# Batches 2 to 6: ScalarE's paired side pieces set in two steps of the scan each, and none in a step in which ScalarE scales a diverted sum

## The chip, the cores and the metric

One core of one Trainium2 chip runs the whole kernel in one launch. The metric is the device time of the launch in microseconds; lower is better. The five engines used are TensorE (PE), VectorE (DVE), ScalarE (ACT), GpSimd (POOL) and SyncE (SP, which only starts DMAs). Each runs its own list of instructions in order, and they meet at semaphores.

## The reference, cut to what matters

The input is 8 sequences of 512 tokens of width 512, in fp32. For each sequence:

```python
xz = einsum('bld,ed->bel', hidden, in_proj_w)      # x and z, 1024 channels each
x = silu(conv(x, 4 taps) + conv_b)
dt_lo, B, C = split(x_proj_w @ x)                  # 32, 16, 16
delta = softplus(dt_proj_w @ dt_lo + dt_proj_b)
for n in 16 states:                                # a scan over the 512 tokens
    h[n] = h[n] * exp(delta * A[:, n]) + delta * B[n] * x
    y += h[n] * C[n]
y = (y + x * D) * silu(z)
x1 = layernorm(hidden + out_proj_w @ y)
out = layernorm(x1 + mixture_of_experts(x1))       # 8 experts, 2 of them per token
```

The experts work on tokens that are sorted by expert: rows are scattered to DRAM, loaded tile by tile, multiplied, stored, and gathered again.

## The kernel before, in words

A batch is one sequence. The scan of a batch is cut in 128 **steps**: step 8n+j is state n (0 to 15) of channel block j (0 to 7), one VectorE scan of 128x512. (The change's own words call such a step a row; here "rows" is kept for lines of the profile.) Batches 2 to 6 share one plan, `SEG_FULL`; batch 0 uses `SEG_PRO`, batch 1 `SEG_TWO`, batch 7 `SEG_EPI`, and the change leaves those three alone. What a step does on each engine:

- **ScalarE**: `decay` (L1784), dA = exp(delta * A) into one of two PSUM buffers. Decay r overwrites the buffer of scan r-2, so it waits until scan r-2 is done. Then, in 7 steps of a batch, `scale_part` (L1767), and then the step's side pieces.
- **GpSimd**: the product dbu (L1925), then its side pieces.
- **VectorE**: in even steps it first adds a sum of the previous transposes to y (`state_part`, L1965, 128x1024), then scan r (L1976), which needs decay r and dbu r, then its side pieces.
- **TensorE**: in even steps it transposes a part of a finished state (L1334, 8 transposes) into one of two buffers hTp; the sum of two steps later reads it. Before that part it waits (`turned_taken`) until ScalarE has taken every side transpose of the earlier steps out of these same buffers.

Of the 64 sums of a batch, 7 are diverted (`BY_DMA`): ScalarE scales the part (128x1024) and a DMA adds it to y, and VectorE skips that sum. The steps of these are 14, 30, 46, 62, 78, 94 and 110.

The **side pieces** are all the other work of three batches at once: the projections and gates of the next batch, the output projection, routing and experts of the one before. `plan` simulates the engines with costs written by hand and returns, for each engine, the list of (step, piece). Each engine works through its own list in order, and where it comes to a piece that is not ready, it stands. ScalarE's pieces that matter here:

- `z i` (exp and copy of a projected gate tile out of PSUM, L1660 and L1666, the copy frees the bank), `z2 i` (ln and exp, L1671 and L1678);
- `x j` (first tap of the convolution from PSUM to u, L1574; VectorE's piece `x j`, L1996, adds the other three taps and frees the bank);
- `sig j` (exp, L1585), `sig2 j` (ln and exp, L1590 and L1597), after which GpSimd multiplies (L1857) and the projection `xproj` on TensorE can start once all eight are done (ScalarE takes it out of PSUM at L1601);
- `dt j` (abs and relu from PSUM, L1624 and L1632; the relu frees the bank), `dt2 j` (exp and ln, L1636 and L1642);
- `ln1 t`, `ln2 t` (three 128x1 operations, `rs`, and the normalization L1544);
- `yT`, `x1T`, `xsT`, `xsL`, `yinit` (copies of side transposes out of hTp, L1684, L1682, L1686, L1680, L1604); `moe`, `moeL` (L1746), `scale` (L1734), `skip` (L1615).

The pairs in brackets run back to back: in a coarse plan such as `SEG_FULL` the first half of a piece calls the second (`if not w.seg.fine: piece(w, ("sig3", j))`). In the fine plans (batches 0 and 1) each half is planned as a piece of its own.

ScalarE's list in the plan of before, where the prediction follows it (a bracket is one step, in order; a star marks a step with `scale_part`):

```
13 [moeL 12, xsL 13]   14* [yT 1]   15 []   16 [xsL 14]
38 []   39 [z 0, z2 0]   40 []   41 [yT 4, yT 5, z 1]
44 [sq2 0]   45 [sum2 1, ln2 0]   46* []   47 [sq2 1, z 2]
51 [sq1 2, z2 2]   52 [ln1 2]   53 [z 3]
72 [x 1, sig 0, sig2 0]   73 [scale 0, sig 1, sig2 1, x 2]
77 [sig 3, sig2 3]   78* [scale 5, x 5, sig 4]
79 [sig2 4, scale 6, x 6, sig 5, sig2 5]   80 [x 7, sig 6, wT]
81 [sig2 6, scale 7, sig 7, sig2 7]   82 []
93 [dt 1, skip 2]   94* [dt2 1]   95 [moe 0]   96 [skip 3]
97 [moe 1, yinit 2, yinit 3]   98 []   99 [dt 2, xsT 2, xsT 3, dt2 2]   100 []
109 [moe 4, dt 5]   110* []   111 [xsT 6, yinit 4, dt2 5]
```

VectorE's pieces there: `x 2` in step 73, `x 5` in 77, `x 6` in 78, `x 7` in 79, each after the scan of its step. TensorE's side transposes: `yT 1` in step 12, `yT 4, 5` in 38, `yinit 2, 3` in 94, `xsT 2, 3` in 96, `yinit 4` in 108.

Of the kernel before, what the change touches and what calls it, by code (L numbers as in the profile page):

```python
# [41 lines left out]
STEPS = NS * ND  # L42
NH = NT
# [45 lines left out]
def last_den(t):  # L89
# [4 lines left out]
SINGLE = {"z": ("z", "z1"), "z2": ("z2", "z3"), "zb": ("zb", "zb1"), "zb2": ("zb2", "zb3"), "sig2": ("sig2", "sig3"), "dt": ("dt", "dt1"), "dt2": ("dt2", "dt3"),  # L94
          "ln1": ("rs1", "ln1"), "ln2": ("rs2", "ln2"), "lnF": ("rsF", "lnF")}
# [253 lines left out]
BY_DMA = [NH * n + 2 for n in range(NS) if n % 2 == 0 and n < NS - 2]  # L349


def by_dma(q, halved=False):

    return not halved and q in BY_DMA
# [170 lines left out]

class Segment:

    def __init__(self, pieces, pace, blocks, next_blocks, steps=STEPS):
        self.fine = any(x[0] in ("dt1", "rs1") for x in pieces)
        self.shares = FINE_SHARES if self.fine else SHARES  # L530
        order, users, turns = plan(pieces, steps, pace, steps > STEPS, self.fine)
# [16 lines left out]
        if steps == STEPS and not self.fine:  # L548
            order["pool"] += [(row + AHEAD - 1, ("hold",) + x, 0) for row, x, _ in order["dve"] if x[0] in STILL and row + AHEAD <= steps]
        self.ends_with_tile = [x for row, x, _ in order["act"]][-1:] == [("moe", LATE - 1)]  # L550
# [185 lines left out]
def build(nc, hid, hidT, w_inT, conv_w, conv_b, w_xT, w_dtT, dt_b, A_log, D, w_outT, gateT, w_expT, exp_b, ident_c, before_c, ramp_c, out):  # L736
    with ExitStack() as ctx:
# [27 lines left out]
        rows = sb("rows", [P, L])  # L765
# [38 lines left out]
        row = sb("row", [P, NT, NE])  # L804
# [710 lines left out]
        def _(act):  # L1515
# [30 lines left out]
            def piece(w, x):  # L1546
                name = x[0]
# [38 lines left out]
                elif name == "sig2":  # L1586
# [4 lines left out]
                    if not w.seg.fine:  # L1591
                        piece(w, ("sig3", j))
# [23 lines left out]
                elif name == "dt":  # L1616
# [8 lines left out]
                    if not w.seg.fine:  # L1625
                        piece(w, ("dt1", j))
# [6 lines left out]
                elif name == "dt2":  # L1633
# [3 lines left out]
                    if not w.seg.fine:  # L1637
                        piece(w, ("dt3", j))
# [8 lines left out]
                elif name in ("z", "zb"):  # L1647
# [13 lines left out]
                    if not w.seg.fine:  # L1661
                        piece(w, (name + "1", i))
# [4 lines left out]
                elif name in ("z2", "zb2"):  # L1667
# [4 lines left out]
                    if not w.seg.fine:  # L1672
                        piece(w, (name[:-1] + "3", i))
# [22 lines left out]
                elif name == "ln1":  # L1696
                    if not w.seg.fine:
                        piece(w, ("rs1", x[1]))
# [9 lines left out]
                elif name == "ln2":  # L1708
                    if not w.seg.fine:
                        piece(w, ("rs2", x[1]))  # L1710
# [28 lines left out]
                elif name in ("moe", "moeL"):  # L1739
                    rows, stored, count = results_of(w, x[1], w.e if name == "moe" else w.d)  # L1740
# [6 lines left out]
                elif name == "wT":  # L1747
                    first, end_t, _ = group_of(x)
# [448 lines left out]
```

## Time and profile before

| | us |
|---|---|
| median of 3 runs (2259.15 to 2264.75) | 2264.38 |
| the profiled execution | 2260.66 |
| its span, first to last instruction | 2258.9 |
| mean length of batches 2 to 6, first scan to first scan | 260.6 |

| engine | busy us | share of the span |
|---|---|---|
| PE | 2036.0 | 90% |
| DVE | 1982.8 | 88% |
| POOL | 1854.5 | 82% |
| ACT | 1658.4 | 73% |

A line of the timeline reads: start in the span, duration, engine, line of the kernel, operation, out<-in, shapes, count (equal neighbours are merged), and in brackets how long the engine stood idle before it and what ended that. Consecutive ScalarE or VectorE operations overlap a little, so what one of them costs is the distance from its start to the next start. The five batches of `SEG_FULL` start at 561.2, 822.1, 1084.6, 1345.1 and 1604.9 us and end at 1864.2; batch 3 (822.1 to 1084.6) is used as the pattern below.

### The profile page before, as it was taken

The page shows a single profiled execution, that of the slowest core. Times are in us where ns is not written, and L with a number is a line of the kernel's source. Part 1 is how long each engine was busy: PE and PEld are TensorE (multiplying, and loading weights), DVE is VectorE, ACT ScalarE, POOL GpSimd, SP SyncE. Part 2 cuts the span into 40 slices and gives each one's busy share as a digit, 9 for nine tenths or more (in the row PEclk, how much of TensorE's full clock was granted, in tenths as well). Part 3 has the DMA queues.
Part 4 walks back from the last instruction along what each step waited for, and adds up shares of the span by engine and source line. Part 5 has one row for each costly group of instructions (what it writes and reads, how often), then busy time and mean ns, then how long its engine had stood idle before and what let it go on. Part 6 is the DMA issues. An engine that isn't in the chain of part 4 may idle for free. (4 is left out here: it accounts for less than half of the span.)

```text
span 2258.9 us, 30428 instructions
## 1 busy us (share of the span) xinstructions
PE 2036.0 (90%) x8624; PEld 1200.9 (53%) x8624; DVE 1982.8 (88%) x2191; ACT 1658.4 (73%) x3074; POOL 1854.5 (82%) x1505
## 2 busy tenths in 40 slices
PE   8897779898999989999899998999899998879898
PEld 3444455455564555545555555645556455655453
DVE  5899989989999999899999999899998998989912
ACT  5767858767598866979588875988678886667534
POOL 2988999788998889889898889989898997696503
PEclk9897879989899999999999999999999999789999
DMA  5432142367754786557863678557855576495775
GB/s 164 160 108 70 40 148 77 95 212 229 246 126 124 231 289 180 137 171 233 280 172 106 209 249 264 118 153 248 293 150 136 176 245 236 146 272 189 246 270 117
DMA packets 222085, 412.79 MB, mean 183 GB/s; under 512 B 29880, under 2 KB 36152, under 8 KB 221920
## 3 DMA queue, kind: packets, MB, share of 16 engines
q1 hardware_dynamic: 180448, 322.36, 42.6%
q0 software_dynamic: 20496, 57.16, 12.4%
q10 hardware_dynamic: 20976, 31.33, 4.3%
q8 instruction: 72, 1.18, 0.2%
q14 instruction: 93, 0.76, 0.1%
HBM read 299.37 MB, written 85.72 MB: 170 GB/s over the span
## 5 line engine op out<-in xcount | busy, mean ns | idle before, releaser
L1784 ACT ACTIVATE dA<-delta,negA 128x512 f32<-128x512 f32 (+1 forms) x1146 | 714.4, 637 | 317.4 <-DVE hst L1976 250.1
L1925 POOL TENSOR_TENSOR hst<-u,Bbc 128x512 f32<-128x512 f32 x666 | 880.7, 1427 | 57.4 <-PE hTp L1334 36.3
L1976 DVE TENSOR_TENSOR_SCAN hst<-dA,hst 128x512 f32<-128x512 f32 x672 | 790.3, 1207 | 44.0 <-ACT dA L1784 36.8
L1334 PEld LDWEIGHTS hTp<-ident,hst 128*128 128x128 f32 x4096 | 496.2, 149 | 318.4 <-issue 172.2
L1334 PE MATMUL hTp<-ident,hst 128*128 128x128 f32 x4096 | 557.9, 288 | 96.5 <-DVE hst L1976 24.4
L1965 DVE SCALAR_TENSOR_TENSOR y<-hTp,Ct,y 128x1024 f32<-128x1024 f32 x463 | 585.1, 1264 | 54.5 <-PE hTp L1334 51.6
L1925 POOL TENSOR_TENSOR first_dbu<-u,Bbc 128x512 f32<-128x512 f32 x222 | 295.1, 1411 | 16.5 <-DVE hits L2057 11.6
L1976 DVE TENSOR_TENSOR_SCAN hst<-dA,first_dbu 128x512 f32<-128x512 f32 x224 | 263.2, 1207 | 17.7 <-issue 9.1
L1318 PE MATMUL bank<-wslot,hidT 128*128 128x512 f32 x512 | 250.3, 621 | 8.1 <-ACT zs L1666 6.2
L1318 PE MATMUL bank<-wslot,tokT 128*128 128x512 f32 x496 | 233.3, 598 | 4.0 <-ACT tokT L1686 3.9
L1318 PE MATMUL bank<-delta,tokT 128*128 128x512 f32 x480 | 224.4, 600 | 0.0
L1318 PE MATMUL bank<-hidT,wslot 128*128 128x512 f32 x384 | 178.1, 601 | 13.6 <-DVE u L1996 13.5
L1996 DVE SCALAR_TENSOR_TENSOR u<-bank,cw,u 128x511 f32<-128x511 f32 (+2 forms) x192 | 142.8, 744 | 31.0 <-ACT u L1574 25.8
L1318 PEld LDWEIGHTS bank<-wslot,hidT 128*128 128x128 f32 x512 | 94.2, 199 | 93.0 <-issue 82.7
L1318 PEld LDWEIGHTS bank<-wslot,tokT 128*128 128x128 f32 x496 | 87.9, 191 | 91.0 <-issue 91.0
L1318 PEld LDWEIGHTS bank<-delta,tokT 128*128 128x128 f32 x480 | 87.1, 195 | 80.0 <-issue 80.0
L1318 PEld LDWEIGHTS bank<-hidT,wslot 128*128 128x128 f32 x384 | 68.6, 191 | 96.3 <-issue 61.5
L1933 POOL TENSOR_TENSOR first_dbu<-u,Bbc 128x512 f32<-128x512 f32 x64 | 82.6, 1348 | 43.2 <-DMA Bbc<-b_scratch 23.4
L1857 POOL TENSOR_TENSOR u<-u,side 128x512 f32<-128x512 f32 x64 | 84.1, 1320 | 38.4 <-ACT side L1597 38.3
L1746 ACT ACTIVATE ysb<-bank 128x512 f32<-128x512 f32 x116 | 68.3, 589 | 62.1 <-PE bank L1318 53.8
L1872 POOL TENSOR_TENSOR zs<-zs,side 128x512 f32<-128x512 f32 x64 | 98.4, 1538 | 16.7 <-ACT side L1678 16.6
L1318 PE MATMUL bank<-wslot,side 128*128 128x512 f32 x224 | 106.5, 601 | 1.9 <-ACT side L1680 1.6
(187 smaller groups left out, 2886.7 us busy)
## 6 DMA issues: line engine op xcount, KB each, us to landing
wslot<-in_w_expT SPq DMA_DIRECT2D x90, 1024.0 KB
Bbc<-b_scratch SPq DMA_DIRECT2D x113, 256.0 KB
wslot<-in_w_inT SPq DMA_DIRECT2D x26, 1024.0 KB
y<-scaled POOLq DMA_DIRECT2D x49, 512.0 KB
zs<-sorted_tokens ACTq DMA_DIRECT2D x91, 256.0 KB, 6.1
sorted_results<-ysb SPq DMA_DIRECT2D x90, 256.0 KB
res<-in_w_expT SPq DMA_DIRECT2D x18, 1024.0 KB, 5.7
gate_scratch<-zs SPq DMA_DIRECT2D x64, 256.0 KB, 2.8
```

The lines of the kernel that those rows point to most:

```text
L1318: mm = nc.tensor.matmul(dst, lhs(k), rhs(k), start=(k == 0), stop=(k == n - 1))
L1334: mm = nc.tensor.transpose(hTp[q % 2][:, tok(j)], hst[n % 2][:, j, start:start + P], ident[:, :])
L1746: nc.scalar.activation(rows, ps[:, :], ACT.Copy).then_inc(bank_taken[s], 1)
L1784: nc.scalar.activation(decay_of(step, halved), delta[w.odd][:, j, cols], ACT.Exp, scale=negA[:, j, n:n + 1]).then_inc(exp_done, 1)
L1857: nc.gpsimd.tensor_tensor(x_j, x_j, side[j % 2][:, :], ALU.mult).then_inc(x_ready, 1)
L1872: nc.gpsimd.tensor_tensor(zs[i % 2][:, :], zs[i % 2][:, :], side[i % 2][:, :], ALU.mult).then_inc(z_ready, 1)
L1925: nc.gpsimd.tensor_tensor(dbu_row(n, j), u[w.odd][:, j, :], Bbc[n % 2][:, :], ALU.mult).then_inc(dbu_done, 1)
L1933: nc.gpsimd.tensor_tensor(half_dbu[k % 4].rearrange("p (k t) -> p k t", k=2), u[w.odd][:, j:j + 2, cols], Bbc[n % 2][:, cols].unsqueeze(1) ...
L1965: nc.vector.scalar_tensor_tensor(y_part, hTp[q % 2][:, :], Ct[odd][:, t, n:n + 1], y_part, ALU.mult, ALU.add).then_inc(acc_done, 1)
L1976: nc.vector.tensor_tensor_scan(hst[n % 2][:, j, :], dA[j % 2][:, :], dbu_row(n, j), 0.0, ALU.mult, ALU.add).then_inc(scan_done, 1)
L1996: tap = nc.vector.scalar_tensor_tensor(late, bank[s][:, 0:L - k], cw[:, j, TAPS - 1 - k:TAPS - k], late, ALU.mult, ALU.add)
```

## The change

The list that the planner made for ScalarE in `SEG_FULL` is rewritten after planning, by `one_by_one`: a piece whose planned step scales a diverted sum moves to the next step; a pair becomes two pieces, the second one step later than the first, unless the list is already behind (then it stays in the same step); and the order of the list is kept, so that a piece behind a moved one is moved with it. The lists of the other engines, and the planner's model, stay as they were. The calls by which the first half of a pair runs the second are switched off in these batches too (`w.seg.single`).

```diff
+SCALED_ROWS = [2 * (q + NH + 1) for q in BY_DMA]
...
+def one_by_one(pieces, steps):
+
+    rows, last = [], 0
+    for row, x, _ in pieces:
+        row += row in SCALED_ROWS
+        for k, name in enumerate(SINGLE.get(x[0], (x[0],))):
+            last = min(max(row + k * (last <= row), last), steps - 1)
+            rows.append((last, (name,) + x[1:], 0))
+    return rows
...
         self.fine = any(x[0] in ("dt1", "rs1") for x in pieces)
+        self.single = self.fine or steps == STEPS
...
+        if self.single and not self.fine:
+            order["act"] = one_by_one(order["act"], steps)
...
-                    if not w.seg.fine:
+                    if not w.seg.single:
                         piece(w, ("sig3", j))
```

The last edit is made at seven places: for `sig3`, `dt1`, `dt3`, `z1`/`zb1`, `z3`/`zb3`, `rs1` and `rs2`.

## Rows read from the trace of the kernel before

**Rows 1.** Busy time of each engine in batch 3 (windows; columns as in its first line).
```profile
core 0: us, PE busy (x) PEld busy (x) DVE busy (x) ACT busy (x) POOL busy (x), PEclk, DMA share, GB/s
822.10:1084.60 262.50, 246.47 (x1070) 146.51 (x1069) 240.81 (x250) 206.74 (x374) 235.57 (x192) 0.95 0.64 198
```

**Rows 2.** VectorE's waits in batches 2 to 6: total us, times, longest.
```profile
DVE hst L1976 <- ACT dA L1784: 35.6, 42, 1.7
DVE y L1965 <- PE hTp L1334: 28.1, 52, 1.0
```

**Rows 3.** ScalarE idle before decays, batches 2 to 6 (line 1784): ended by, us, times.
```profile
  DVE hst L1976: 164.2, 204
```

**Rows 4.** ScalarE's timeline in steps 78 and 79 of batch 3.
```profile
980.30 0.71 ACT L1734 ACTIVATE spare<-res,mix 128x512 f32<-128x512 f32 x1
980.91 0.76 ACT L1574 ACTIVATE u<-bank,cb,cw 128x512 f32<-128x512 f32 x1
...
982.09 0.68 ACT L1784 ACTIVATE dA<-delta,negA 128x512 f32<-128x512 f32 x1
982.70 0.62 ACT L1590 ACTIVATE side<-side 128x512 f32<-128x512 f32 x1
983.36 0.63 ACT L1597 ACTIVATE side<-side 128x512 f32<-128x512 f32 x1
983.89 0.71 ACT L1734 ACTIVATE zs<-res,mix 128x512 f32<-128x512 f32 x1
```

**Rows 5.** VectorE's timeline in steps 77 and 78 of batch 3.
```profile
980.61 1.22 DVE L1976 TENSOR_TENSOR_SCAN hst<-dA,hst 128x512 f32<-128x512 f32 x1
981.74 2.29 DVE L1996 SCALAR_TENSOR_TENSOR u<-bank,cw,u 128x511 f32<-128x511 f32 x3
983.95 1.21 DVE L1976 TENSOR_TENSOR_SCAN hst<-dA,hst 128x512 f32<-128x512 f32 x1
```

**Rows 6.** ScalarE's timeline in step 99 of batch 3.
```profile
1029.98 0.68 ACT L1632 ACTIVATE delta<-bank,dtb 128x512 f32<-128x512 f32 x1
...
1030.55 1.08 ACT L1686 ACTIVATE tokT<-hTp 128x512 f32<-128x512 f32 x2
```

**Rows 7.** VectorE's timeline in steps 98 to 100 of batch 3.
```profile
1029.21 1.28 DVE L1965 SCALAR_TENSOR_TENSOR y<-hTp,Ct,y 128x1024 f32<-128x1024 f32 x1 [0.47 <-PE hTp L1334]
1030.41 2.33 DVE L1976 TENSOR_TENSOR_SCAN hst<-dA,hst 128x512 f32<-128x512 f32 x2
1033.30 1.28 DVE L1965 SCALAR_TENSOR_TENSOR y<-hTp,Ct,y 128x1024 f32<-128x1024 f32 x1 [0.56 <-PE hTp L1334]
```

**Rows 8.** TensorE's timeline in steps 96 and 98 of batch 3.
```profile
1031.29 1.10 PE L1318 MATMUL bank<-res,tokT 128*128 128x512 f32 x2 [1.24 <-ACT tokT L1686]
1032.22 1.91 PE L1334 MATMUL hTp<-ident,hst 128*128 128x128 f32 x16
```

**Rows 9.** TensorE's and then VectorE's timeline after step 14 of batch 3.
```profile
848.65 1.94 PE L1334 MATMUL hTp<-ident,hst 128*128 128x128 f32 x8 [2.44 <-ACT tokT L1684]
...
850.63 1.28 DVE L1965 SCALAR_TENSOR_TENSOR y<-hTp,Ct,y 128x1024 f32<-128x1024 f32 x1 [0.28 <-PE hTp L1334]
```

**Rows 10.** TensorE (step 40) and VectorE (steps 46, 53, 73) of batch 3, timeline.
```profile
895.33 1.94 PE L1334 MATMUL hTp<-ident,hst 128*128 128x128 f32 x16 [0.39 <-ACT tokT L1684]
...
905.14 1.22 DVE L1976 TENSOR_TENSOR_SCAN hst<-dA,hst 128x512 f32<-128x512 f32 x1 [1.42 <-ACT dA L1784]
...
919.22 1.22 DVE L1976 TENSOR_TENSOR_SCAN hst<-dA,hst 128x512 f32<-128x512 f32 x1 [0.91 <-ACT dA L1784]
...
968.20 1.53 DVE L1996 SCALAR_TENSOR_TENSOR u<-bank,cw,u 128x511 f32<-128x511 f32 x2 [1.57 <-ACT u L1574]
```

**Rows 11.** TensorE at the start of xproj (batch 5) and ScalarE at its end.
```profile
1521.21 2.81 PE L1318 MATMUL bank<-u,hidT 128*128 128x512 f32 x6 [1.29 <-POOL u L1857]
...
1530.11 0.59 ACT L1601 ACTIVATE rows<-bank 64x512 f32<-64x512 f32 x1 [1.11 <-PE bank L1318]
```

**Rows 12.** TensorE's timeline at the part of step 110 of batch 3.
```profile
1054.41 1.06 PE L1334 MATMUL hTp<-ident,hst 128*128 128x128 f32 x8 [0.34 <-ACT y L1604]
```

More of the change, by code:

```diff
@@ L1624, in piece @@
                     nc.scalar.activation(a, ps[:, :], ACT.Abs, bias=dtb[:, j:j + 1]).then_inc(sp_step, 1)
-                    if not w.seg.fine:
+                    if not w.seg.single:
                         piece(w, ("dt1", j))
@@ L1636, in piece @@
                     nc.scalar.activation(a, a, ACT.Exp, scale=-1.0).then_inc(sp_step, 1)
-                    if not w.seg.fine:
+                    if not w.seg.single:
                         piece(w, ("dt3", j))
@@ L1660, in piece @@
                     nc.scalar.activation(a, ps[:, :], ACT.Exp, scale=-1.0).then_inc(zsig_step, 1)
-                    if not w.seg.fine:
+                    if not w.seg.single:
                         piece(w, (name + "1", i))
@@ L1671, in piece @@
                     nc.scalar.activation(a, a, ACT.Ln, bias=1.0).then_inc(zsig_step, 1)
-                    if not w.seg.fine:
+                    if not w.seg.single:
                         piece(w, (name[:-1] + "3", i))
@@ L1696, in piece @@
                 elif name == "ln1":
-                    if not w.seg.fine:
+                    if not w.seg.single:
                         piece(w, ("rs1", x[1]))
@@ L1708, in piece @@
                 elif name == "ln2":
-                    if not w.seg.fine:
+                    if not w.seg.single:
                         piece(w, ("rs2", x[1]))
```

## The prediction

> **What bounds the kernel now.** I read the windows first: in batch 3, VectorE is busy 240.8 of 262.5 us, more than ScalarE (206.7) and GpSimd (235.6) [rows 1]; TensorE's 246.5 is modelled and holds matmuls that wait for banks. So VectorE sets the pace, step by step, and what counts is its idle time, 21.7 us in this batch. The waits say what ends it: over batches 2 to 6, 35.6 us in 42 waits are for a decay dA from ScalarE, 28.1 us in 52 are for transposed parts from TensorE [rows 2]. The first is what the change can touch: at most 7.1 us of a batch.
>
> The third view speaks against it. ScalarE stands before its decays 164.2 us in 204 waits, for VectorE's scan [rows 3]. So in a third of the 640 steps ScalarE is as far ahead as two dA buffers allow. There, a side piece that stands before a decay runs in time in which ScalarE would wait anyway; the same piece behind that decay starts only after scan r-2. Splitting does not spread work over idle time, it pushes it behind a gate. Whether that costs depends on who waits for the piece.
>
> **The change, part by part.** It adds and removes no instruction (batches 2 to 6, 32 pairs in each). Costs of ScalarE from start to start: decay 0.61, scale 0.61 (980.30 to 980.91, 982.09 to 982.70), second half of `sig2` 0.53, taken as 0.54 (983.36 to 983.89) [rows 4]; relu of `dt` 0.57, two copies of transposes 1.08 [rows 6]. A first tap takes 0.76 to its end [rows 4].
>
> *Decays that come earlier (gain).* In step 46 VectorE waits 1.42 us, in step 53 0.91 us [rows 10]. Step 46: `ln2 0`'s second half leaves step 45, so decay 46 comes earlier; but it then stands between decay 46 and decay 47, and decay 47 comes no earlier. Nothing is gained there. Step 53: `ln1 2`'s normalization leaves step 52; the 0.91 go. Against this, step 40: `z 0` now has one operation in step 39 and three in step 40, behind a decay that waits for scan 38; `yT 4` and `yT 5`, in step 41, come about 1.1 us later, and TensorE's part started 0.14 us after them (895.33, released by the copy) [rows 10], with only 0.3 or so to spare for VectorE's sum: a loss of 0.8. What is left, some 0.1 to 0.5 us gained, meets step 73: there VectorE waits 1.57 us for `x 2` [rows 10], and `x 2` moves to step 74, behind one more decay (0.61). I take steps 37 to 76 together as 0; ends: 1.5 us gained if the losses are covered, 1 us lost if the gain is.
>
> *Step 15.* `yT 1` leaves the starred step 14 and runs behind decay 15. TensorE's next part started when that copy was out, and VectorE's sum waited for the part, 0.28 us [rows 9]. The copy comes one decay later: +0.6 us, and the earlier decay 15 buys nothing, since the sum is later.
>
> *Steps 77 and 78, the largest term.* Follow `one_by_one`: `sig2 3` gives its second half to step 78, so `scale 5`, `x 5` and `sig 4` (moved out of the starred step) stand in 79; then `sig2 4` is split, and `scale 6`, `x 6` and all behind stand in 80. VectorE's list was not touched: it wants `x 5` in step 77 and `x 6` in step 78. So VectorE, having done scan 77, waits for a piece that stands behind decay 79, which waits for scan 77. No one is deadlocked, but nothing overlaps: after scan 77 come decay 0.61, scale 0.61, tap 0.76 and two hand-overs of 0.03 to 0.05: 2.1 us idle, where now the taps start the moment the scan is over (981.74) [rows 5]. Then after scan 78: decay 0.61, second half of `sig2 4` 0.54, scale 0.61, tap 0.76, hand-overs: 2.6, of which 0.1 exists now (the scan ends at 985.16, 983.95 + 1.21 [rows 5]): 2.5 us. `x 7` is not late: three taps and scan 79 (2.29 + 1.2 [rows 5]) cover its 3.3 us of ScalarE. Sum +4.6 us. Bounds: not below 4.0, since both chains hang on VectorE's own scans; up to 6 if TensorE, idle meanwhile, is slow after it.
>
> *Step 82, xproj.* `sig3 6`, `scale 7`, `sig 7` and `sig2 7` stand behind decay 82, which waits for scan 80, where four of them ran before it. Eight gates must be multiplied before `xproj`; TensorE starts it at the moment the last is out (1.29 us of waiting, released by GpSimd) and ScalarE waits 1.11 us for its end [rows 11]. I work out that the last gate comes 2.3 us later; the parts of two steps that lie between cover some of it at step 88: +1.5 us, between 0 (in batches in which TensorE was late itself) and 2.3.
>
> *Steps 96 to 100.* With `dt 1`'s relu moved behind decay 94 its bank comes free later, ScalarE idles before decay 94 and has some 1.1 us more to do before `yinit 3`, for which part 96 waits: sum 98, which waits 0.47 us already [rows 7], is later by 1.2. Then step 99: only `dt 2`'s first half is left in it; the relu, `xsT 2` and `xsT 3` stand behind decay 100, which waits for scan 98. After that scan: decay 0.61, relu 0.57, copy 0.6 [rows 4, 6], matmuls of the expert tile 0.93 (1031.29 to 1032.22, started by the copy) [rows 8], part until its sum 1.08 (1032.22 to 1033.30) [rows 7, 8]: 3.8 to 3.9 us, of which scan 99 (1.13) covers its share: 2.8 idle where 0.56 is now [rows 7]: +2.2. Bounds of both together: 1.5 to 4.
>
> *Steps 106 to 112.* Decay 109 and the starred step 110 get `dt1 4` to `dt3 4` and `dt1 5` in front; part 110 waits for the copy `yinit 4` [rows 12], which comes about 0.75 later; with 0.25 at step 106: +1.0, between 0 and 2.
>
> The sum for a batch: 0 + 0.6 + 4.6 + 1.5 + 3.4 + 1.0 = 11.1 us; five batches 55.5. The profiled execution took 2260.66 us, so it would take 2316.2; the median of the runs lies 3.7 above it, and I predict from the median: 2264.4 + 55.5 = 2319.9.
>
> A rule that speaks for the change: in the second half of `sig2`, which needs the first, ScalarE waits for its end: 0.66 from start to start (982.70 to 983.36) against 0.53 where the next needs nothing (983.36 to 983.89) [rows 4]. With a decay between them 0.13 us is saved, 4 us of ScalarE in a batch. The Trainium skill, "ScalarE: Activation LUTs", What ACT_TABLE_LOAD costs, has independent activations overlapping by about 93 ns; by that figure it is 3 us in a batch. Either lands in time in which ScalarE waits anyway, except before steps 47 and 53.
>
> **The rivals.** *A, faster*: what VectorE waits for is a burst of ScalarE, in front of one decay, and halving the bursts removes it. Place: steps 15, 46, 53, 95, price 35.6 us at most [rows 2]; it decides if the displaced pieces all have a taker who is later than the decay. Half of the waits gone and nothing lost: 2264.4 - 18 = 2246. For it: 42 waits for dA. Against: rows 3, and that two of VectorE's takers are certain to be late.
>
> *B, slower by less*: only the chains of steps 77 and 78 and of step 100 are real (6.8 us), half of it is made up by what VectorE now waits for (step 88, the sums), and the rest is hidden: 5 us a batch, 2289.
>
> *C, slower by more*: TensorE's clock. Part 14, after 2.44 us of idle TensorE, took 1.94 us for 8 transposes [rows 9], where 8 matmuls more in the same time are usual, as in 1.91 us for 16 [rows 8]: the lower of the two levels, 1.2 instead of 2.4 GHz. The new stalls leave TensorE idle in steps 78 to 80 and 99 for over 2 us each; if what follows runs at the lower level and VectorE waits for it, each costs up to 1 us more, and other waits grow: 16 us a batch, 2344. The Trainium skill, "TensorE: Matmul & The Clock Gate", What's actually happening, says that an idle array falls to half its clock; the trace agrees in the row named.
>
> *D, nothing*: the plan has slack at each place, 2264.
>
> **How the numbers follow.** Forecast 0.62, B 0.18, C 0.10, A 0.07, D 0.03. The likeliest gives 2320. The bounds of the terms make 2290 (A's gains in steps 37 to 76, xproj hidden, lower ends) to 2338; the range takes in B: 2288 to 2340. A change of 0.3% (7 us) is about what can be told from none. Slower by more: 0.62 + 0.18 + 0.10 = 0.90; within: 0.03; faster: 0.07.
>
> **What would show it.** Right: ScalarE's waits before the decays grow; VectorE gets ten new waits for `u` (L1574), of 2.1 and 2.5 us, beside the five of step 73; its waits for hTp grow by some 20; waits for dA fall from 35.6 to below 25; batches of 271 to 272 us in place of 260.6, batches 0, 1 and 7 unchanged. Wrong: no wait over 2 us for `x 5` and `x 6`, or batches as long as before.

## The result, and the profile after

The changed kernel takes 2344.11 us (median of 4 runs, 2334.11 to 2345.86), the kernel before 2264.57 beside it (4 runs, 2259.15 to 2268.25): ratio 1.0344, interval 1.0308 to 1.0381. The forecast was slower, 2320, between 2288 and 2340. The direction is right. The time lies 24 us above the forecast and 4 us outside the range; it is the 2344 that rival C gave, to which I had left a chance of 0.10.

The page of the changed kernel, profiled in an execution of 2345.75 us (lines of the code are those of before plus 17):
```profile
span 2344.0 us, 30428 instructions
PE 2066.5 (88%) x8624; PEld 1213.9 (52%) x8624; DVE 1985.2 (85%) x2191; ACT 1644.7 (70%) x3074; POOL 1852.6 (79%) x1505
...
L1801 ACT ACTIVATE dA<-delta,negA 128x512 f32<-128x512 f32 (+1 forms) x1146 | 719.4, 638 | 401.5 <-DVE hst L1993 333.9
...
L1982 DVE SCALAR_TENSOR_TENSOR y<-hTp,Ct,y 128x1024 f32<-128x1024 f32 x463 | 585.3, 1264 | 105.7 <-PE hTp L1351 101.1
```
The number of instructions is what it was, and so, nearly, is VectorE's busy time (1982.8 before, 1985.2 after): the 85 us by which the profiled executions differ (2345.75 against 2260.66) are waits. ScalarE does not work more either, it stands more in front of its decays. The windows of batches 0 to 6, one after the other, say where:
```profile
core 0: us, PE busy (x) PEld busy (x) DVE busy (x) ACT busy (x) POOL busy (x), PEclk, DMA share, GB/s
56.30:301.50 245.20, 190.83 (x766) 115.69 (x766) 233.10 (x217) 179.64 (x293) 222.37 (x182) 0.86 0.31 90
301.50:561.50 260.00, 235.23 (x1020) 139.91 (x1020) 239.00 (x249) 189.66 (x329) 221.79 (x184) 0.93 0.50 157
561.50:837.80 276.30, 244.01 (x1048) 144.40 (x1049) 241.68 (x249) 203.41 (x372) 237.17 (x193) 0.94 0.59 181
837.80:1114.00 276.20, 245.41 (x1070) 144.79 (x1069) 241.93 (x251) 204.02 (x374) 235.06 (x192) 0.96 0.61 188
1114.00:1392.50 278.50, 251.60 (x1070) 149.24 (x1069) 240.76 (x251) 204.38 (x374) 235.81 (x192) 0.94 0.61 187
1392.50:1672.40 279.90, 251.47 (x1070) 149.16 (x1069) 240.67 (x251) 204.41 (x374) 235.36 (x192) 0.94 0.61 185
1672.40:1950.70 278.30, 249.81 (x1067) 147.67 (x1066) 239.52 (x250) 203.27 (x373) 233.97 (x191) 0.94 0.60 185
```
Batches 0 and 1 are as long as before (245.3 and 260.0 us against 245.7 and 258.9, from scan 0 to scan 0 in the trace). Batches 2 to 6 take 276.1 to 279.9 us, 277.8 in the mean, where they took 260.6: 17.2 us more in each, with VectorE as busy as in [rows 1]. The granted clock of the last two batches falls from 0.98 to 0.94.

VectorE's waits in batches 2 to 6:
```profile
DVE y L1982 <- PE hTp L1351: 74.3, 64, 4.6
DVE hst L1993 <- ACT dA L1801: 34.1, 35, 1.8
DVE u L2013 <- ACT u L1591: 31.2, 20, 2.6
DVE hst L1993 <- issue: 18.6, 9, 2.9
```
Against [rows 2], the waits for transposed parts grow by 46 us (28.1 to 74.3), and those for decays stay: 34.1 where it was 35.6. The waits for first taps grow from 6.4 us in 5 to 31.2 in 20, and those whose releaser the trace doesn't show from 5.8 us to 18.6. What the change was to win was not there.

**Steps 77 and 78 of batch 3**, VectorE's timeline and then ScalarE's:
```profile
1002.12 2.31 DVE L2013 SCALAR_TENSOR_TENSOR u<-bank,cw,u 128x511 f32<-128x511 f32 x3 [2.07 <-ACT u L1591]
1004.35 1.21 DVE L1993 TENSOR_TENSOR_SCAN hst<-dA,hst 128x512 f32<-128x512 f32 x1
1008.15 2.32 DVE L2013 SCALAR_TENSOR_TENSOR u<-bank,cw,u 128x511 f32<-128x511 f32 x3 [2.59 <-ACT u L1591]
```
```profile
1000.08 0.69 ACT L1801 ACTIVATE dA<-delta,negA 128x512 f32<-128x512 f32 x1 [1.10 <-DVE hst L1993]
1000.71 0.71 ACT L1751 ACTIVATE spare<-res,mix 128x512 f32<-128x512 f32 x1
1001.32 0.76 ACT L1591 ACTIVATE u<-bank,cb,cw 128x512 f32<-128x512 f32 x1
...
1005.60 0.69 ACT L1801 ACTIVATE dA<-delta,negA 128x512 f32<-128x512 f32 x1 [2.33 <-DVE hst L1993]
1006.23 0.61 ACT L1614 ACTIVATE side<-side 128x512 f32<-128x512 f32 x1
1006.74 0.71 ACT L1751 ACTIVATE zs<-res,mix 128x512 f32<-128x512 f32 x1
1007.36 0.76 ACT L1591 ACTIVATE u<-bank,cb,cw 128x512 f32<-128x512 f32 x1
```
Read the two together. ScalarE stands for 1.10 us until scan 77 is out, then decay 79, the scale and the first tap run one by one, and VectorE, whose next work is the other taps of `x 5`, stands all that time. Then the same with decay 80, the second half of `sig2 4`, scale and tap. This is the chain of the forecast, link by link.

**Step 99**, TensorE's timeline, then VectorE's:
```profile
1057.95 2.04 PE L1335 MATMUL bank<-res,tokT 128*128 128x512 f32 x2 [3.54 <-ACT tokT L1703]
1059.79 2.43 PE L1351 MATMUL hTp<-ident,hst 128*128 128x128 f32 x16
```
```profile
1061.39 1.28 DVE L1982 SCALAR_TENSOR_TENSOR y<-hTp,Ct,y 128x1024 f32<-128x1024 f32 x1 [4.29 <-PE hTp L1351]
```
The two matmuls behind the copies took 1.10 us and the 16 transposes 1.91 in [rows 8]; now 2.04 and 2.43, and the idle time ahead of them is 3.54 us in place of 1.24. Over just this stretch the granted clock is 0.64, and 1.00 in the same work of before:
```profile
1057.90:1062.00 4.10, 4.05 (x18) 2.94 (x19) 0.61 (x1) 2.73 (x5) 2.37 (x2) 0.64 0.72 260
```
```profile
1031.20:1034.00 2.80, 2.71 (x19) 2.21 (x20) 2.24 (x3) 2.77 (x6) 2.80 (x4) 1.00 1.01 370
```
(The first is of the changed kernel, the second of the kernel before.)

To see all of a batch I put every idle time of VectorE to the step in which it lies, from scan to scan, and took means over batches 2 to 6. A cell gives single steps and their waits (8: 1.12 is a wait of 1.12 us in step 8), before and then after in the same order. This table, worked out from the two traces, is what the rest is measured against (us a batch; an interval of steps holds all of its waits, not only those named, and the sum is made of unrounded values):

| steps | before | after | more, in the interval | forecast |
|---|---|---|---|---|
| 0 to 36 | 8: 1.12, 9: 0.36, 15: 0.93, 17: 0.42 | 1.45, 1.03, 1.51, 0.74 | +1.9 | +0.6 |
| 37 to 76 | 41: 0, 46: 1.40, 47: 0.39, 49: 0.48, 53: 0.91, 62: 0.53, 63: 1.83, 66: 1.74 | 0.71, 0.37, 1.09, 1.09, 0, 0.01, 3.39, 1.15 | +0.9 | 0 |
| 77, 78 | 0.07, 0.21 | 2.14, 2.66 | +4.5 | +4.6 |
| 81 to 88 | 81: 0.43, 85: 0, 88: 0.46 | 1.28, 0.67, 1.48 | +2.6 | +1.5 |
| 95 to 99 | 97: 0.47, 99: 0.56 | 1.50, 4.52 | +4.8 | +3.4 |
| 105 to 117 | 105: 0.95, 110: 0.12, 111: 1.38 | 1.73, 1.99, 0.23 | +1.9 | +1.0 |
| sum | | | +16.5 | +11.1 |

### The profile page after: what moved, and what is told of

It is laid out like the page before. It is cut to its first block, busy times and chain, and to the rows that moved or that the text cites. A ratio compares the mean times of both kernels' runs of the same rounds, so it can differ in the third digit from the quotient of the medians.

```text
span 2344.0 us, 30428 instructions
## 1 busy us (share of the span) xinstructions
PE 2066.5 (88%) x8624; PEld 1213.9 (52%) x8624; DVE 1985.2 (85%) x2191; ACT 1644.7 (70%) x3074; POOL 1852.6 (79%) x1505
## 4 chain that ended last, share of the span: by engine, by line
POOL 28%; PE 28%; DVE 16%; issue 12%; ACT 8%; DMA 6%; SPq 1%; DVEq 0%; ACTq 0%; POOLq 0%
PE bank L1335 19%; POOL hst L1942 13%; DVE hst L1993 7%; PE hTp L1351 6%; POOL first_dbu L1942 4%; DVE y L1982 3%; DVE u L2013 3%; ACT dA L1801 2%; POOL delta L1916 2%; DVE hst L2158 2%; DMA spare<-gate_scratch 2%; POOL u L1919 2%; POOL zs L1889 1%; POOL first_dbu L1950 1%; DMA Bbc<-b_scratch 1%
## 5 line engine op out<-in xcount | busy, mean ns | idle before, releaser
L1801 ACT ACTIVATE dA<-delta,negA 128x512 f32<-128x512 f32 (+1 forms) x1146 | 719.4, 638 | 401.5 <-DVE hst L1993 333.9
L1993 DVE TENSOR_TENSOR_SCAN hst<-dA,hst 128x512 f32<-128x512 f32 x672 | 788.9, 1206 | 44.7 <-ACT dA L1801 31.2
L1351 PEld LDWEIGHTS hTp<-ident,hst 128*128 128x128 f32 x4096 | 503.0, 150 | 321.8 <-issue 171.7
L1351 PE MATMUL hTp<-ident,hst 128*128 128x128 f32 x4096 | 563.6, 290 | 96.8 <-DVE hst L1993 23.5
L1335 PE MATMUL bank<-wslot,hidT 128*128 128x512 f32 x512 | 252.1, 624 | 15.7 <-ACT zs L1683 13.9
L1916 POOL TENSOR_TENSOR delta<-delta,hidT 128x512 f32<-128x512 f32 x56 | 74.5, 1330 | 62.0 <-ACT hidT L1659 62.0
L1335 PE MATMUL bank<-wslot,side 128*128 128x512 f32 x224 | 111.3, 624 | 1.8 <-ACT side L1697 1.5
L1889 POOL TENSOR_TENSOR zs<-zs,side 128x512 f32<-128x512 f32 x64 | 98.3, 1536 | 16.5 <-ACT side L1695 16.4
```

The source lines that it names most:

```text
L1335: mm = nc.tensor.matmul(dst, lhs(k), rhs(k), start=(k == 0), stop=(k == n - 1))
L1351: mm = nc.tensor.transpose(hTp[q % 2][:, tok(j)], hst[n % 2][:, j, start:start + P], ident[:, :])
L1801: nc.scalar.activation(decay_of(step, halved), delta[w.odd][:, j, cols], ACT.Exp, scale=negA[:, j, n:n + 1]).then_inc(exp_done, 1)
L1889: nc.gpsimd.tensor_tensor(zs[i % 2][:, :], zs[i % 2][:, :], side[i % 2][:, :], ALU.mult).then_inc(z_ready, 1)
L1916: nc.gpsimd.tensor_tensor(d, d, third(w, j), ALU.add).then_inc(delta_ready, 1)
L1993: nc.vector.tensor_tensor_scan(hst[n % 2][:, j, :], dA[j % 2][:, :], dbu_row(n, j), 0.0, ALU.mult, ALU.add).then_inc(scan_done, 1)
```

## The experiments

Two readings of the extra 6 us a batch stood against each other. One says that all of it is order: more pieces than I counted stand behind a gated decay. The other says that part of it comes with the stalls: TensorE, idle for longer, works at its half clock afterwards, and a wait taken away at one place turns up at the next. The first four kernels apply the change in one range of steps each, so that the places can be priced and added; the others take single causes away. Each is compared with runs of the kernel before that were made beside it, whose medians differ somewhat (2255.91 to 2264.57 us), so kernels of different groups are compared by their ratios and not by their times.

**The change in steps 0 to 36, 37 to 71, 72 to 87 or 88 to 127 alone.** The edit, with the range of each kernel in the first line:
```diff
-        row += row in SCALED_ROWS
+        late = 72 <= row < 88
+        row += late and row in SCALED_ROWS
...
-            last = min(max(row + k * (last <= row), last), steps - 1)
+            last = min(max(row + late * k * (last <= row), last), steps - 1)
```
Steps 0 to 36:

> The rewriting of ScalarE's list is kept for the pieces planned in steps 0 to 36 alone (in batches 2 to 6); all later steps run as in the kernel before. Theory 1 (each loss is a chain of its own, a piece behind a gated decay with a taker that waits, and the chains add up): the part of step 16 is late by one copy, 0.6 us in a batch, and what the trace of the changed kernel shows at steps 8, 9 and 17 (1.3 us in a batch) was handed on by the end of the batch before and is not there: 3 us over five batches, about 2268. Theory 2 (what the prediction missed is one effect of the whole: a longer idle TensorE runs at its lower clock everywhere): this part alone leaves the clock as it was, 3 us too, but then the four parts together fall 20 us or more short of the whole change. Theory 3 (the waits of steps 8 and 9 belong to this part): 9 us, 2274.

Measured: 2260.15 us (10 runs) against 2255.91 before (19 runs), ratio 1.0009 (0.9990 to 1.0028), which can't be told from none. Step 15 went from 0.93 to 1.60 us, as forecast; the waits of steps 8 and 9 grew by 0.2 us together, not by 1.0. So what those have more in the whole change does not come from these steps; theory 3 falls.

Steps 37 to 71:

> Only the pieces planned in steps 37 to 71 are rewritten (z pairs, ln pairs, steps 46 and 62). Theory 1: the waits of the changed kernel's trace in these steps come with it: 0.7 at step 41, 0.6 at 49 and 1.6 at 63 lost, 1.0 at 46/47 and 0.9 at 53 gained less 0.7: +1.0 us in a batch, 5 us over all, 2269. Theory 2: the steps give back what they lose, as predicted: 2264 within 3 us.

Measured: 2265.03 us (10 runs), ratio 1.0042 (1.0019 to 1.0066), between 0.9 and 3 us a batch, so a loss as in theory 1. Step 41 has 0.71 us more, 46 0.94 less, 47 0.70 more, 49 0.95 more, 53 0.91 less, as the prediction had it for each but 49; and step 63 has 1.26 more, which the prediction lacked (the expectation above took it from the trace of the changed kernel) and which is what makes the sum positive.

Steps 72 to 87:

> Only the pieces planned in steps 72 to 87 are rewritten (sig pairs, and scale, x, sig moved with them). Theory 1: VectorE waits 2.1 us for x 5 and 2.7 us for x 6 in each batch, and xproj starts later: 4.6 + 2.5 = 7 us in a batch, 35 us over all, 2300. Theory 2 (xproj is hidden as long as TensorE keeps its clock): 4.6 + 0.5, 26 us, 2290. Theory 3 (x 5 and x 6 are late only because of pieces pushed on from earlier steps): under 10 us.

Measured: 2302.61 us (4 runs), ratio 1.0193 (1.0161 to 1.0225), 9 us a batch and so more than the 7 of theory 1. The waits of 77 and 78 are 2.14 and 2.66 us in all five batches. Step 81 has 2.59 where it had 0.43, and steps 8 and 9 have 1.1 more.

Steps 88 to 127:

> Only the pieces planned in steps 88 to 127 are rewritten (dt pairs, steps 94 and 110). Theory 1: sum 98 is late by 1.0, sum 100 by 4.0, and steps 105 to 111 lose 1.5: 6.5 us in a batch, 33 us over all, 2297. Theory 2 (sum 100 is late by its own chain of 2.2 us only, the other 1.8 us come from a TensorE that the earlier parts had let cool down): 4.6 us in a batch, 23 us, 2288. In both, TensorE's granted clock after step 99 tells: at 1.2 GHz there under theory 1, at 2.4 GHz under theory 2.

Measured: 2291.39 us (4 runs), ratio 1.0154 (1.0129 to 1.0179), 7 us a batch: theory 1. The four excesses, 0.0009, 0.0042, 0.0193 and 0.0154, add up to 0.0398, where the whole change has 0.0344: a difference that the intervals of the five ratios leave room for. So the places are nearly independent, and half of the loss is in steps 72 to 87, two fifths in 88 to 127.

This kernel also shows the clock without another cause beside it. Of its five batches, four wait 4.27 to 4.64 us in step 99, and batch 4 waits 2.86. TensorE's timeline and windows in batch 3 and in batch 4:
```profile
1037.97 2.05 PE L1336 MATMUL bank<-res,tokT 128*128 128x512 f32 x2 [3.54 <-ACT tokT L1704]
1039.81 2.63 PE L1352 MATMUL hTp<-ident,hst 128*128 128x128 f32 x16
```
```profile
1302.37 1.10 PE L1336 MATMUL bank<-res,tokT 128*128 128x512 f32 x2 [3.54 <-ACT tokT L1704]
1303.30 1.91 PE L1352 MATMUL hTp<-ident,hst 128*128 128x128 f32 x16
```
```profile
1037.90:1042.00 4.10, 4.03 (x16) 2.92 (x17) 0.40 (x1) 2.74 (x5) 2.36 (x3) 0.59 0.76 290
1302.30:1306.40 4.10, 4.03 (x25) 3.01 (x26) 2.02 (x2) 2.74 (x5) 2.36 (x2) 1.00 0.77 282
```
The same work after the same idle time, at a granted clock of 0.59 and of 1.00 over the stretch, and VectorE's sum waits 4.48 us in the one and 2.86 in the other.

**The change without the move out of the scaling steps.**
```diff
-        row += row in SCALED_ROWS
```

> The changed kernel without its move out of the starred steps (the line that adds one to a piece's step where ScalarE scales a diverted sum); the pairs are still split. Theory 1 (the second half behind the gate is what costs): x 5 is back in step 78 and not late, the copy yT 1 is back in step 14; x 6 still stands behind decay 80, xsT 2 and 3 behind decay 100, the second halves of dt 4 behind decay 108. 2.1 + 0.7 us a batch are saved of 17: about 2.7% over the kernel before. Theory 2 (the move out of the starred steps is what costs, since it pushes all that follows): under 1% over the kernel before.

Measured: 2333.19 us (4 runs) against 2257.24 (10 runs), ratio 1.0326 (1.0289 to 1.0363). Step 77 waits 0.32 us in place of 2.14, step 15 0.69 less and 97 0.52 less, 95 0.52 more; the chain of step 78 and that of step 99 stand. So the cost stays with the split (theory 1), but the time saved is less than expected: 1.0326 against the 1.0344 of the whole change can't be told apart.

**The change without the split**: the move out of scaling steps alone, both halves of a pair in one step.
```diff
-            last = min(max(row + k * (last <= row), last), steps - 1)
+            last = min(max(row, last), steps - 1)
```

> The changed kernel with its move out of the starred steps, but both halves of a pair in the same step. Theory 1: x 5 waits 2.1 us for decay 79, x 6 does not wait, since it stands in step 79 with x 5; the sum of step 16 is 0.7 late; in step 95 VectorE's wait for the decay goes, and comes back at the sum of step 98 because the two copies yinit come no earlier: 2.8 us a batch, 0.6% over the kernel before. Theory 2: most of the 3.4%.

Measured: 2268.85 us (7 runs), ratio 1.0048 (1.0020 to 1.0076). Step 77 waits 2.14 us, 81 1.88, 97 1.56, but 99 only 0.16, and 95 0.36 where 1.57 was. The split is what costs, as theory 1 had it; the move alone costs about a seventh of the whole, though it makes one of the two chains by itself.

**The taker moved with its piece.** The changed kernel, with VectorE's `x 5`, `x 6` and `x 7` one step later:
```diff
+            order["dve"] = [(row + (x in (("x", 5), ("x", 6), ("x", 7))), x, share) for row, x, share in order["dve"]]
+            order["dve"].sort(key=lambda p: p[0])
```

> The changed kernel, with VectorE's pieces x 5, x 6 and x 7 set one step later (78, 79, 80), so that scan 78 runs while ScalarE does decay 79, scale 5 and x 5. Theory 1 (the loss is that VectorE asks before ScalarE may answer): the waits of 2.14 and 2.66 us become about 1.0 and 0.5, 3.3 us a batch, and the stretch at the lower clock in steps 80 to 82 gets shorter: 17 to 25 us less than the changed kernel, about 2.5% over the kernel before. Theory 2 (ScalarE is simply too busy in these steps): the waits move on to x 6 and x 7 and the time stays at 3.4%.

Measured: 2336.20 us (4 runs, 2317.59 to 2340.03), ratio 1.0324 (1.0264 to 1.0383), so no gain that can be told. VectorE's waits from 302 us on, in the changed kernel and then in this one:
```profile
DVE u L2013 <- ACT u L1591: 34.3, 21, 3.2
...
DVE res L2138 <- PE bank L1483: 11.5, 9, 2.1
```
```profile
DVE res L2140 <- PE bank L1485: 32.6, 23, 2.2
...
DVE u L2015 <- ACT u L1593: 15.7, 16, 3.2
```
The waits for taps halved (34.3 to 15.7 us), the waits for TensorE's banks of the weights to be spread (`res`) took their place (11.5 to 32.6). In steps, 77 fell from 2.14 to 0 and 78 from 2.66 to 1.02, while 80 rose from 0 to 2.51 and 81 from 1.28 to 3.05. Theory 1, that a later taker would simply get these waits back, fell here. TensorE's timeline of batch 3 shows what the later taps make late themselves:
```profile
1012.68 3.01 PE L1485 MATMUL bank<-w_rows,rows 64*128 64x512 f32 x4 [2.42 <-DVE u L2015]
...
1017.52 3.78 PE L1485 MATMUL bank<-w_rows,rows 64*128 64x512 f32 x4
```
VectorE's last taps free the bank into which TensorE spreads the weights. Now that they are a step later, TensorE stands 2.42 us for that bank where it stood 1.12 in the changed kernel, and the two groups of four matmuls behind it take 3.01 and 3.78 us where each took 1.98 there; the granted clock from 1012.60 to 1021.30 is 0.55. VectorE waits for these matmuls.

**TensorE kept at work before step 99.**
```diff
+                if w.seg is SEG_FULL and x == ("xsT", 3):
+                    pe.wait_ge(acc_done, sums(w.b, parts + 1))
+                    for j in range(24):
+                        nc.tensor.transpose(hTp[parts % 2][:, tok(j % ND)], ident[:, :], ident[:, :])
```

> The changed kernel, with 24 more transposes of the identity on TensorE in each of batches 2 to 6, after the side transposes of step 96 and the sum of step 98, into the buffer hTp that is free then: they fill some 2.6 of the 3.5 us for which TensorE stands before moe 2. They compute nothing that is used. Theory 1 (of the 4.5 us of waiting in step 99, 2.8 are the chain and the rest is TensorE's lower clock after the idle time): the wait in step 99 falls to 2.8 in every batch, and that of step 105 to 1.1: 8 to 10 us less than the changed kernel. Theory 2 (the chain itself is that long, the clock has nothing to do with it): no change, or some us more.

Measured: profiled run 2326.68 us against the changed kernel's 2345.75; median 2331.54 (4 runs), ratio 1.0329 (1.0292 to 1.0365). The medians cannot tell 1.0329 from 1.0344, so the 8 to 10 us of theory 1 do not show in them; the trace shows the place. TensorE at step 99 of batch 3, and VectorE's sum:
```profile
1052.22 2.84 PE L1397 MATMUL hTp<-ident 128*128 128x128 f32 x24 [0.51 <-DVE y L1986]
1055.26 1.10 PE L1335 MATMUL bank<-res,tokT 128*128 128x512 f32 x2 [0.20 <-ACT tokT L1707]
1056.19 1.91 PE L1351 MATMUL hTp<-ident,hst 128*128 128x128 f32 x16
```
```profile
1057.27 1.28 DVE L1986 SCALAR_TENSOR_TENSOR y<-hTp,Ct,y 128x1024 f32<-128x1024 f32 x1 [2.86 <-PE hTp L1351]
```
With 24 transposes in the idle time the two matmuls take 1.10 us again, and VectorE waits 2.86 us in all five batches, where the mean was 4.52. Step 105, which had 2.07 to 2.20 in batches 4 to 6 and 1.08 in batches 2 and 3, has 1.08 in all. (TensorE works at full clock there in both kernels, granted 1.00. In batches 4 to 6 of the changed kernel the 16 transposes of step 99 take 3.4 us, in batches 2 and 3 2.4 to 2.5, and TensorE is still behind when it comes to step 105.) So of the 3.96 us that step 99 has more, 1.66 are the half clock (4.52 - 2.86), and 2.30 the order of the pieces. Of the 19 us by which the two profiled executions differ, these two steps are 11.5.

**Steps 76 to 82 left as they were**, all else changed:
```diff
+        late = not 76 <= row < 83
+        row += late and row in SCALED_ROWS
...
+            last = min(max(row + late * k * (last <= row), last), steps - 1)
```

> The changed kernel with the pieces planned in steps 76 to 82 left as in the kernel before (sig, x and scale there run as pairs and in their own steps). Theory 1 (the losses of steps 77 to 88 are the chains behind decays 79, 80 and 82 and TensorE's lower clock after them, all started here): VectorE's waits in steps 77 and 78 go, and steps 81 to 88 together wait no more than in the kernel before: 8 to 9 us less in a batch, 40 to 45 us less than the changed kernel, 1.5 to 1.7% over the kernel before. Theory 2 (the waits of steps 81 to 88 come from steps before 76): 4.6 us a batch, 2.4% over the kernel before.

Measured: 2298.83 us (4 runs) against 2258.31 (23 runs), ratio 1.0185 (1.0140 to 1.0229). The batches take 268.0 us in the mean of the profiled execution, 9.8 less than in the changed kernel; by the ratios it is 7 us a batch. VectorE's waits for taps, batches 2 to 6, are nearly those of before again (8.3 us, 6.4 before):
```profile
DVE y L1983 <- PE hTp L1352: 61.6, 55, 4.6
...
DVE u L2014 <- ACT u L1592: 8.3, 10, 1.9
```
The waits of 77, 78, 81 and 85 are gone together (0.07, 0.21, 0 and 0 us), and that of 88 falls from 1.48 to 0.22. Of the 9.8 us, 8.2 are waits of steps 77 to 94. Another 1.4 lie in steps 95 to 117, where the rewriting is the same in both kernels: two batches in which step 99 found TensorE at full clock waited 2.86 us there, the other three 4.28 to 4.64. So the delays of these seven steps are worth about half of the 17.2 us.

**Step 107 left as it was**, so that the relu and the last operation of `dt2 4` stay together:
```diff
+        late = not 107 <= row < 108
```
(the other lines as in the kernel above).

> The changed kernel with dt 4 and dt2 4 (step 107) left as pairs. Theory 1 (step 110 waits 2.0 us because GpSimd gets the last half of dt2 4, which stands behind decay 108, too late and has the products of steps 110 and 111 behind it): the wait of step 110 falls under 0.5, that of step 111 rises to some 1.1 by the copy yinit 4, about 1 us less in a batch. Theory 2 (step 110 is late by ScalarE's decay and the scaled sum): 2.0 stays.

Measured: one execution, 2327.19 us. Step 110 went from 1.99 to 0.00 us, step 111 from 0.23 to 1.71. GpSimd's timeline before step 110 of batch 3, in the changed kernel and then in this one:
```profile
1077.83 1.27 POOL L1916 TENSOR_TENSOR delta<-delta,hidT 128x512 f32<-128x512 f32 x1 [5.28 <-ACT hidT L1659]
1079.18 1.27 POOL L1919 TENSOR_TENSOR u<-delta,u 128x512 f32<-128x512 f32 x1
1080.41 2.50 POOL L1942 TENSOR_TENSOR hst<-u,Bbc 128x512 f32<-128x512 f32 x2
```
```profile
1074.86 1.27 POOL L1917 TENSOR_TENSOR delta<-delta,hidT 128x512 f32<-128x512 f32 x1 [2.36 <-ACT hidT L1660]
```
GpSimd stands 5.28 us for the last operation of `dt2 4`, and the product that scan 110 needs comes behind it: so the wait of step 110, whose releaser VectorE's own row does not show (`issue`), is GpSimd's. But what step 110 gives back is taken in step 111, by decay 111 (0.72) and by the part behind it (0.99), as it was before the change (0.39 and 0.99): 0.5 us net, half of what theory 1 had. (The execution is 18.6 us shorter than the profiled one of the changed kernel; the rest of that lies in steps that this edit does not touch, 8, 9, 105 and 117 among them, whose waits vary between batches.)

**The gains alone.** If some waits can be had without a late taker, this should beat the kernel before: four pieces that stand in front of something VectorE waits for are moved, nothing else. From the kernel before:
```diff
+LATER = {("yT", 1): 13, ("ln2", 0): 47, ("ln1", 2): 54}
...
+        if steps == STEPS and not self.fine:
+            order["act"] = sorted([(LATER.get(x, row), x, share) for row, x, share in order["act"]], key=lambda p: (p[0], p[1] == ("moe", 3)))
```

> The kernel before (not the changed one), with four pieces of ScalarE moved by what the studies show: yT 1 from the starred step 14 to the end of step 13; ln2 0 whole from step 45 to 47, behind the two decays that VectorE waits for; ln1 2 whole from 52 to 54; and in step 105 the copies xsT 4 and 5 ahead of moe 3. Theory 1 (a piece is to stand where its taker has most time, in whichever direction): waits of steps 15 to 17 fall by 0.7, of 46 and 47 by up to 1.8, of 53 by 0.9, of 105 by 0.4; some comes back at step 50 and at the gate: 1.5 to 3 us a batch, 8 to 15 us, 0.3 to 0.7% faster than before. Theory 2 (ScalarE is full from step 37 to 53, and what it puts off comes back at once; upstream gains are lost at step 73, where ScalarE waits for a store): within 0.2% of before.

Measured: 2260.60 us (12 runs) against 2258.31 (23 runs), ratio 1.0016 (0.9999 to 1.0033). The moves do win where they were aimed (step 15 0.54, 17 0.42, 46 1.06, 53 0.91, 66 1.08), and it is given back: 48 and 49 take 0.50 and 0.72, step 105 takes 0.92, since `moe 3` now frees its bank later for TensorE's part, and steps 8 and 9 take 1.5. The gain of 0.3 to 0.7% is not there; theory 2 stands.

**Two of the moves** (`LATER = {("yT", 1): 13}` and the order in step 105):

> The kernel before with yT 1 moved from step 14 to the end of step 13 and, in step 105, xsT 4 and 5 ahead of moe 3, and nothing else. Theory 1: part 14 of TensorE starts 1.6 us earlier and no longer after an idle stretch: 0.7 us in steps 15 to 17 and 0.4 in step 105, 5 us over all, 0.2%. Theory 2: decay 14 is late by the copy (0.3 us) and takes it back: no difference.

Measured: 2262.35 us (12 runs), ratio 1.0026 (1.0008 to 1.0043), slightly slower where theory 1 had slightly faster. Step 105's 0.92 is there again, and it takes back the 0.54 and 0.42 won in steps 15 and 17. In the profiled execution (2256.61 us, the fastest of the twelve) VectorE idles 20.7 us a batch against 20.9 before, so where the 0.3% of the medians lies is open. No kernel of this study beats the one before.

## Why the prediction was wrong in size

**Right.** VectorE is the bound, ScalarE's idle time before its decays is not free capacity but a gate [rows 3], and a piece put behind that gate is as late as scan r-2. *Steps 77 and 78*: forecast idle 2.1 and 2.6 us, measured 2.14 and 2.66 in each of five batches; +4.6 against +4.5. *Step 15*: +0.6, measured +0.58, and +0.67 alone. *Step 97* (sum 98): +1.2, measured +1.04. *Steps 41, 46, 47 and 53*: 0.8 lost, nothing gained between 46 and 47, 0.91 gone; measured +0.71, -1.03 and +0.70 (0.3 gained), -0.91. ScalarE's idle time before decays grew (250.1 to 333.9 us in all), and the waits for parts grew by more than the 20 us foreseen. *What hangs on rows 4*, the 0.13 us saved between the two halves of `sig2`, gained nothing that shows: ScalarE's work is smaller by 14 us (1658.4 to 1644.7) and VectorE waits for it as before. (The Trainium skill, "ScalarE: Activation LUTs", What ACT_TABLE_LOAD costs, gives the 93 ns for back-to-back activations and does not set dependent ones apart; that a dependent one starts 0.13 us later is in [rows 4] alone.)

**The step that failed first: step 99, "2.8 idle where 0.56 is now: +2.2".** The chain was right, 2.86 us wherever TensorE works at full clock. But I took the matmuls at 0.93 us and the part at its price of [rows 7, 8], prices of the upper level, after an idle time that the same forecast made three times as long. At the lower of the two levels (granted 0.5, 1.2 in place of 2.4 GHz) the two matmuls and the part cost VectorE 1.66 us more, in the mean of the batches: measured +3.96, and +5.0 with step 97, outside the 1.5 to 4 given for both. I had seen the effect and its row [rows 9] and put it into rival C, with 0.10, as if it excluded the forecast. It did not: C's premise, TensorE idle for over 2 us in steps 78 to 80 and 99, was the forecast's own result. Two things that hold together were given chances as if only one could. The Trainium skill ("TensorE: Matmul & The Clock Gate", What's actually happening), which I had cited, says the idle array drops to half its clock; the windows above agree with 0.64 and 0.59 against 1.00, though one batch in five kept 1.00 after the same idle time. By the run with TensorE kept at work, the clock of step 99 costs 2.3 us a batch, 1.66 there and 0.65 in step 105, where TensorE is still behind. That is half of the 4.9 by which C stood above the forecast, a sum that C did not derive term by term; in steps 81 to 88 the clock decides what a single batch waits, but has little part in the mean difference (below). So C's number came true by its mechanism only in part.

**Steps 81 to 88, "+1.5, between 0 and 2.3".** Measured +2.6. The last gate was as late as I had worked out: `xproj` starts 6.5 us after the end of scan 80 in all five batches. In the kernel before it starts 3.9 us after it (5.0 in batch 3); so the gate is 2.6 us later, and the forecast had 2.3. What it did not have is what TensorE's clock does there, and that little of the delay is covered. In batch 3 TensorE waits 3.84 us for the last gate, and then four matmuls take 3.75 us where six took 2.81 [rows 11]:
```profile
1022.62 3.75 PE L1335 MATMUL bank<-u,hidT 128*128 128x512 f32 x4 [3.84 <-POOL u L1874]
```
```profile
1028.38 1.28 DVE L1982 SCALAR_TENSOR_TENSOR y<-hTp,Ct,y 128x1024 f32<-128x1024 f32 x1 [1.59 <-PE hTp L1351]
```
(TensorE at the start of xproj and VectorE's sum after it, changed kernel.) But [rows 11] are of a batch in which `xproj` ran at full clock, and before the change that held for only two of the five. The same stretch in batch 4 and in batch 5 of the kernel before:
```profile
1259.00:1264.00 5.00, 4.97 (x12) 2.41 (x13) 5.00 (x5) 2.64 (x4) 5.00 (x5) 0.66 1.04 320
1521.20:1526.00 4.80, 4.79 (x17) 2.62 (x18) 4.80 (x5) 2.62 (x4) 4.80 (x5) 1.00 1.03 315
```
In steps 81 to 91 of the kernel before, VectorE waited 0 us in batches 5 and 6 and 1.4 and 1.5 us in batches 2 and 4, which differ from them in this clock. In the changed kernel `xproj` began at the lower clock in all five batches, and they wait 3.8 to 4.4 us there. In batches 4 to 6 the four matmuls that spread the weights just ahead of it ran at the lower clock too (3.78 us for 1.98), and that is where step 81 waits 2.0 to 2.4 us; in batches 2 and 3 it is step 85 that waits, 1.8 and 1.6. Batches with the lower clock in `xproj` alone, 2 and 3 of the changed kernel and 2 and 4 of the one before, differ by 2.8 us, the whole delay of the gate: the 0.8 us of cover that I had taken off was not there. Batches 5 and 6, which had the full clock before, lose more (from 0 to 3.8 and 4.1 us), and batch 3, where TensorE was slow ahead of `xproj` already, loses less (from 3.3 to 4.2); in the mean the two nearly cancel. With the delays of steps 76 to 82 gone, three batches wait 0 again, and the two with `xproj` at the lower clock 1.1.

**Steps 37 to 76, "together as 0".** Measured +0.9. The terms of steps 41, 46, 47 and 53 were right. Step 73, where `x 2` now stands behind one more decay, waits no longer than it did (1.26, before 1.36). Places without a term moved both ways: steps 49 (+0.6), 63 (+1.6) and 70 (+0.4) against 62 (-0.5) and 66 (-0.6). The largest, step 63, the traces explain: in step 62 ScalarE scales a diverted sum, and for that it waits 0.86 us for TensorE's part, in every batch, and before the change in none; decay 63 stands behind the scale, and VectorE waits 1.62 us for it:
```profile
952.60 1.11 ACT L1784 ACTIVATE scaled<-hTp,Ct 128x1024 f32<-128x1024 f32 x1 [0.86 <-PE hTp L1351]
```
```profile
954.85 1.22 DVE L1993 TENSOR_TENSOR_SCAN hst<-dA,hst 128x512 f32<-128x512 f32 x1 [1.62 <-ACT dA L1801]
```
I looked at what the moved pieces make late on VectorE and TensorE, and not at ScalarE itself waiting for TensorE in a starred step.

**Steps 106 to 112, "+1.0, between 0 and 2".** Measured +1.9 with step 105. The size is within the bounds, the place is not: I named the part of step 110 and the copy `yinit 4`; the wait is for GpSimd's product, behind the last operation of `dt2 4`. GpSimd appeared in no term of the forecast except xproj.

**Steps 8 and 9: no term.** +1.0. The kernel with steps 0 to 36 alone has only 0.2 of it, those with 72 to 87 and with 88 to 127 have 1.1 each, which speaks for lateness carried over the end of the batch. It is not shown: the kernel with TensorE kept at work and the one with step 107 left have all the rest of the change and only 0.3 and 0.2, and the wait of step 8 varies from 0 to 2.4 us between batches of one execution. The cause stays open.

**Waits for decays "fall to below 25".** They are 34.1. That of 53 went and that of 46 shrank, those of 47, 63 and 88 grew.

In sum, of the 5.4 us a batch by which the table's 16.5 exceed the forecast's 11.1, 2.3 are the half clock of step 99 (with step 105), 1.1 are in steps 81 to 88, 1.3 are in steps 8, 9 and 17, and 0.9 in steps 37 to 76; the other terms were 0.2 too high. The range was also narrower than its own terms: the bounds written beside them (0.6 for step 15, which has none), added up, give 4.6 to 15.9 us a batch, which is 2287 to 2344, and not 2290 to 2338; the measured 2344.11 lies at the end of that sum.

*Rival A* has its answer too: waits for decays can be removed one by one, as in the kernel with four moves, but as much comes back within a few steps or at the start of the next batch. *Rival B*'s cover, half made up by other waits, was not there: the four ranges add up to more than the whole by only 0.0054. (Its 5 us a batch is also not half of its 6.8, which would be 3.4, or 2281.)

## What to carry to other kernels

Idle time of an engine in front of a gated instruction is capacity only for work placed ahead of that instruction; work moved behind it waits for the gate, so move a piece only where its taker has slack, and look at every engine that takes it, the moving one among them. Where your own forecast leaves TensorE idle for longer, price the work that follows at its lower clock in the same sum instead of keeping that as a rival. Moving the taker later is no cure by itself: what the taker frees comes later too, and the wait goes there. And add the bounds of the terms up before giving a range.

## What the runs showed of the hardware that was not expected

The same 3.54 us of idle TensorE, before the same two matmuls in the same program, was followed by a granted clock of 1.00 in one batch and by the lower level in the other four (0.59 over the stretch in batch 3); so an idle time of this length does not decide the clock by itself, and a wait behind it is either 2.86 or 4.3 to 4.6 us, from batch to batch. A much shorter one does not either: in the kernel before, 1.28 us of idle TensorE ahead of `xproj` was followed by a granted clock of 0.66 in batch 4 and 1.29 us by 1.00 in batch 5. And 24 transposes of a constant, 2.84 us of TensorE, are enough to keep it at the upper level there in all five batches.
